# Attention stage of a macaron layer: order of the uses of one PSUM bank

## What is computed

```python
x = x + 0.5 * _L0_ffn_ref(_layernorm(x), ...)
x = x + _L0_attn_ref(_layernorm(x), ...)      # normalizes again, with ln_scale and ln_bias
x = x + 0.5 * _L0_ffn_ref(_layernorm(x), ...)

# _L0_attn_ref, h normalized:
c_q, c_kv = h @ w_down_q.T, h @ w_down_kv.T           # latents of 128
q, k, v = c_q @ w_up_q.T, c_kv @ w_up_k.T, c_kv @ w_up_v.T   # 16 heads of 64
q, k = rope(q), rope(k)
out = softmax(q k^T / 8) v;  out = out @ w_out.T + residual
```

## Time and profile before

| | |
|---|---|
| median of three runs | 4095.92 us (4093.1 to 4099.3) |
| profiled execution | 4098.04 us, span 4096.1 us |
| PE busy, whole span | 3897.4 us (95%), weight loads 2207.7 us (54%) |
| POOL, DVE, ACT busy | 2932.8 (72%), 2849.5 (70%), 2536.2 us (62%) |
| attention stage | about 520 to 3590 us |

### The profile page before, as it was taken

How to read it: one execution, slowest core, us unless ns; L and a number is a source line. 1 busy time by engine, 2 the same in 40 slices (tenths; PEclk the granted TensorE clock), 3 DMA queues, 4 the chain that set the end, 5 groups by cost and what they waited for, 6 DMA issues and landing times. The chain is left out here.

```text
span 4096.1 us, 65749 instructions
## 1 busy us (share of the span) xinstructions
PE 3897.4 (95%) x24908; PEld 2207.7 (54%) x24908; DVE 2849.5 (70%) x3796; ACT 2536.2 (62%) x3191; POOL 2932.8 (72%) x1632
## 2 busy tenths in 40 slices
PE   7999979999999999999999999999999999989999
PEld 6888834444444444444444444444444444478888
DVE  5656567777777776777778777767776777565563
ACT  4455446766766676667666766766676666645544
POOL 3444448878877897888788878878887888634443
PEclk9999989999999999999999999999999999999999
DMA  3233221111211221121122212211211121142331
GB/s 123 99 124 109 81 93 53 60 55 59 83 53 53 71 66 53 61 81 53 53 66 76 63 53 66 68 50 60 86 55 53 58 79 62 33 145 76 125 114 63
DMA packets 192772, 300.36 MB, mean 73 GB/s; under 512 B 50328, under 2 KB 100937, under 8 KB 191817
## 3 DMA queue, kind: packets, MB, share of 16 engines
q1 hardware_dynamic: 192456, 296.17, 22.3%
HBM read 201.20 MB, written 26.73 MB: 56 GB/s over the span
## 5 line engine op out<-in xcount | busy, mean ns | idle before, releaser
L1088 DVE TENSOR_REDUCE atNM<-atPS 128x2 f32<-128x1024 f32 x1024 | 1225.7, 1219 | 452.8 <-PE atPS L899 450.1
L1029 ACT ACTIVATE atPT<-atPS 128x1024 f32<-128x1024 f32 x1024 | 1014.0, 1024 | 773.1 <-PE atPS L920 766.7
L1187 POOL TENSOR_TENSOR atACC<-atACC,atPT 128x1024 f32<-128x1024 f32 x510 | 1238.7, 2429 | 89.3 <-ACT atPT L1029 39.1
L931 PE MATMUL atPO<-atPT,atV 128*64 128x512 f32 x4096 | 1014.2, 602 | 0.0
L1187 POOL TENSOR_TENSOR atACC<-atPT 128x1024 f32<-128x1024 f32 x255 | 606.6, 2379 | 262.8 <-PE atOT L953 181.7
L1020 ACT ACTIVATE atPS<-atSH 128x1024 f32<-128x1024 f32 x683 | 687.4, 1023 | 50.8 <-DVE atNM L1088 34.0
L920 PE MATMUL atPS<-atQH,atKL 64*128 64x512 f32 x2048 | 459.9, 445 | 66.3 <-DVE atPS L1094 51.7
L931 PEld LDWEIGHTS atPO<-atPT,atV 128*64 128x64 f32 x4096 | 259.0, 136 | 456.5 <-issue 433.1
L899 PE MATMUL atPS<-atKH,atQH 64*128 64x512 f32 x2048 | 444.0, 431 | 10.0 <-ACT atQH L1009 7.9
L1094 DVE COPY atPS<-atSH 128x1024 f32<-128x1024 f32 x341 | 418.7, 1228 | 37.9 <-DMA atSH<-atMD 11.4
L920 PE MATMUL atPS<-atQH,atKH 64*128 64x512 f32 x2048 | 406.6, 393 | 0.0
(11 more groups left out here) (278 smaller groups left out, 6461.5 us busy)
## 6 DMA issues: line engine op xcount, KB each, us to landing
atSH<-atMD SPq DMA_DIRECT2D x128, 512.0 KB, 4.3
atVT<-atR SPq DMA_DIRECT2D x508, 128.0 KB, 2.1
f1GB<-f1GD SPq DMA_DIRECT2D x128, 256.0 KB, 6.7
f2GB<-f2GD SPq DMA_DIRECT2D x128, 256.0 KB, 6.8
atRSUM<-atRD SPq DMA_DIRECT2D x126, 256.0 KB, 4.0
X<-x SPq DMA_DIRECT2D x4, 1024.0 KB, 6.0
XS<-x SPq DMA_DIRECT2D x16, 256.0 KB, 3.6
x<-X SPq DMA_DIRECT2D x16, 256.0 KB, 2.3
```

Source lines behind the costliest of these rows:

```text
L931: ins = pe.eng.matmul(PO[HI[h], :], V[n % 2][:, j, HI[h]], PT[k % NPT][:, h, :], start=j == 0, stop=j == T - 1)
L1029: act.eng.activation(PT[k % NPT][:, :, :], PS[ring.of[step]][:, :, :], ACT.Exp, scale=SCALE).then_inc(grown.sem)
L1088: dve.eng.tensor_reduce(NM[:, q // 4, :, q % 4, t], PS[ring.of[step]][:, :, :], AX.X, ALU.max, negate=True).then_inc(most_out.sem)
L1187: pool.eng.tensor_tensor(total[:, :, :], begun[:, :, :], PT[k % NPT][:, :, :], ALU.add).then_inc(gathered.sem)
```

## The change

Two things. A function `apart` looks at the tail of each pass: where the list at x + 1 has a raise and the list at x + 2 has any use of OT, the raise is taken out of its place between the two fills and put at the end of the pass, behind that use. And the last four entries of TURNS, for the second half of a batch, move: turns from periods -9 early and -9 late to -13 late and -12 late, latents from -8 early and -8 late to -9 late and -8 late.

```diff
-            TURNS = [(-21, late), (-20, late), (-17, early), (-17, late), (-9, early), (-9, late), (-8, early), (-8, late)]
+            TURNS = [(-21, late), (-20, late), (-17, early), (-17, late), (-13, late), (-12, late), (-9, late), (-8, late)]
@@
+            def uses(steps):
+
+                return [s for s in steps if s[0] in ("turn", "latent", "raise", "value", "row", "sum", "outward")]
+
+            def apart(one, two):
+
+                raised = [s for s in one if s[0] == "raise"]
+                if raised and uses(two):
+                    return [s for s in one if s not in raised], two + raised
+                return one, two
@@
-                order += others_of(x) + held + tile("attend", x - 1)
-                order += gathers(held + tile("attend", x - 1))
+                now = held + tile("attend", x - 1)
+                order += others_of(x) + now + gathers(now)
@@
-                order += tile("fill", x + 3) + others_of(x + 1) + tile("fill", x + 4) + now + gathers(now) + others_of(x + 2)
+                one, two = apart(others_of(x + 1), others_of(x + 2))
+                order += tile("fill", x + 3) + one + tile("fill", x + 4) + now + gathers(now) + two
```

## The result

The changed kernel takes 4137.6 us (median of 4 runs, 4136.2 to 4144.1) against 4097.0; the ratio is 1.0102, 95% interval 1.0088 to 1.0117. It is slower by 41 us; 4128 with a range of 4102 to 4146 was forecast. In the changed file every line behind the new functions stands 12 further down: 878 is now 890, 953 is 965, 1014, 996 and 1041 are 1026, 1008 and 1053.

The account below looks back on a forecast made before the run. PE's own matmul sequence was taken to bound the attention stage; 7.2 + 22.1 + 6.0 + 3.6 + 7.6 + 1.2 - 13.4 - 2.2 = +32 us on a median of 4095.9 gave 4128 us, range 4102 to 4146.

Parts of the forecast that it names:

- The frame: Attention stage, 520 to 3590 us: PE's own matmul sequence sets the time; an added stall counts unless later waits recover it.
- Rival 1: Slips of PE are taken back by shorter later waits for DVE fills: at most 23 us, 4105 us; chance 0.18.
- Case B: 21 tails, raise moved directly behind a row, waiting for ACT's copy after both fills: +1.05 each, +22.1 us.
- Case A: 20 tails, raise moved directly behind a sum, waiting for ACT's copy after both fills: +0.36 each, +7.2 us.
- the difference stays: Sum-then-raise tails with DVE late: fills and old wait are late together, so +0.36 still holds.
- case C: Five tails, two attends between raise and turn before; raise now directly behind the turn: 5 x 1.19, +6.0 us.
- case D: Five tails, one attend between raise and turn before; raise now directly behind the turn: +3.6 (two tails), +7.6 (three).
- four new turns with a raise two attends behind: Turn's copy falls between the two fills; bounds 0 and 0.78, 0.3 taken for each, +1.2 us.
- Turns and latents: Seven batches: two of three waits behind out-projections vanish, 14 x 0.96, -13.4; waits for fills used up, -2.2 us.
- new turns in slots with a wait for a fill: Five new turns land where PE waits for a DVE fill anyway, using up 0.45 each: -2.2 us.
- Cover: SyncE's later swap DMAs, POOL's rotate and DVE's raise operations stay covered after the move; nothing counted.
- margin of 0.1: DVE behind a moved raise: fill ready after 4.9 us, PE needs it after some 5.0; nothing counted.

Follow-up runs that it names:

- row run: Kernel before with old periods, a raise moved behind only where the later use is a row (21 tails): 4118.9 us, ratio 1.0049.
- the swap: Kernel before, raise and sum of a tail change places: 4081.1 us, ratio 0.9961; with the new periods 4071.5 (0.9935), on another chip 4068.9 (0.9931).

## Why the prediction was right, point by point

**The frame.** PE's own sequence sets the time and slips are not taken back: held. The row run moves 21 raises, loses 22.6 us in these tails and 20.2 in the stage, and nothing comes back in the passes directly behind (-0.1 us). Rival 1 (4105) would have given back about 0.45 a tail. The low share of weight loads, which spoke for it, did not show slack here: in an attend, matmuls start in pairs every 0.43 us, and the weight loads beside them take 0.14 of it.

**Case B, +22.1.** Measured +22.5 in the profiled run, 1.05 to 1.09 a tail for a forecast of 1.05; alone, +20 by the ratio. The mechanism is shown by the copy moved on ACT.

**Case A, +7.2.** Fourteen tails cost 0.28 to 0.45 for a forecast of 0.36, one nothing, and five 0.7 to 1.5, so that the sum is 10.8. The five are tails in which DVE was late and PE now stands still for 2.2 to 2.5 us. Two things failed there. In two of them (1.46 and 1.30) PE's clock is low inside the tail (below). In the other three (0.71, 0.76, 1.13) "the difference stays" is what failed: DVE's subtraction ahead of the reductions (line 1083, now 1095) took 2.77, 2.55 and 2.54 us where it had taken 2.48, 2.19 and 1.82 before, so the late tails are not late by the same amount in both executions, and the excess over 0.36 is about that difference.

**Cases C and D.** For the ten tails together, the moved turns included, the forecast comes to 6.0 + 3.6 + 7.6 + 5 x 0.58 = 20.1; measured 21.0. That this fits so well is partly luck. Without the turns' own time case C is 4.4 for 6.0 and case D 13.7 for 11.2. The waits themselves are as worked out: in the first D tail the raise starts 4.00 us after its old place, for 4.04 forecast, and in the C tail at 774.20 the next score comes 4.52 after that place, for 4.49. But three of the five C passes had a stall of some 0.55 ahead of their tail that is gone in this execution, and four of the five D tails have a low clock in them or behind them. The four new turns with a raise two attends behind cost about 0.7 each, not 0.3: with 0.78 as the upper bound I had gone for the wrong end; +1.6.

**Turns and latents, -13.4 and -2.2.** The passes that lost a turn or a latent gave -21.9, of which 14 x 0.58 = 8.1 is the turns' own time: -13.8; the latents among them only change places. The new turns in slots with a wait for a fill cost nothing, where 0.13 each had been left. The periods alone gave -13.9. That one latent per batch stays behind an out-projection was right, seven waits.

**Cover.** SyncE and POOL: right, no wait of PE for either came up. DVE behind the moved raise, with the margin of 0.1: held. The passes directly behind the 21 rows of the row run do not grow. Those behind the five D tails grew by 3.6 us in all, but by 0.5 to 1.4 only behind the four with a low clock, and by -0.01 behind the one without; in the run with `apart` alone, whose two D tails have no low clock, it is 0.01 in sum.

**Sum.** 32 forecast, 41 measured, at the upper end of the forecast's own range of 4115 to 4138; the sign, the mechanism and the sizes of the main terms hold. The largest thing missing is PE's clock, for which the sum has no term. A stretch of 3.4 us at the lower clock costs 1.4 to 1.6 us (below); the profiled execution after has nine of them between 620 and 3590 us, that before has three, so about 9 of its 42.8 us are the clock (an estimate, 6 x 1.5). The run with `apart` alone checks the rest: it has three such stretches like the kernel before, and its stage grew by 35.9 us, where the forecast's terms for it, 7.2 + 22.1 + 3 x 1.19 + 2 x 1.82, add up to 36.5.

## What to carry to other kernels

Before a use of a shared bank is moved right behind another, look up which engine empties the bank and what stands in that engine's queue at that moment; the wait is not only the copy's 0.3 to 0.8 us but also the time until the copy's turn comes. A listed wait is not a gain in reserve: work that lay ahead of it was free, and moving that work behind the wait's place pays for it anew. The cure for a bank passed from hand to hand is distance and a place in an idle stretch of the emptying engine, here the sum ahead of the first fill with two attends behind it, 16 us on top of the exchange of places and, with the new periods, 46 us in all against the kernel before.

## What the hardware showed that I had not expected

A wait of about 2 us or more can cost more than itself. After the wait of 2.34 us for a turn's copy, the raise ran in 1.98 us; in the same kind of tail at 1990.74, behind a wait as long, in 1.08:

```profile
830.07 0.66 PE L872 MATMUL atOT<-ident,Y 128*128 128x128 f32 x4
833.06 1.98 PE L890 MATMUL atOT<-atCKV,WK 128*64 128x512 f32 x4 [2.34 <-ACT atHT L1008]
834.97 0.80 PE L932 MATMUL atPS<-atQH,atKL 64*128 64x512 f32 x2
...
1990.74 1.08 PE L890 MATMUL atOT<-atCKV,WK 128*64 128x512 f32 x4 [2.33 <-ACT atHT L1008]
```

The granted clock of PE in such stretches of the kernel after (length, busy us of PE, PEld, DVE, ACT, POOL, clock, DMA share, GB/s):

```profile
833.00:836.40 3.40, 3.34 (x10) 1.46 (x12) 1.29 (x2) 0.01 (x1) 0.51 (x1) 0.50 0.00 0
...
1307.00:1313.00 6.00, 5.14 (x18) 2.43 (x18) 2.41 (x3) 1.83 (x3) 1.48 (x1) 0.54 0.11 44
...
2311.00:2314.00 3.00, 2.64 (x8) 0.94 (x10) 0.62 (x2) 1.28 (x3) 0.53 (x1) 0.50 0.03 5
2707.00:2710.00 3.00, 2.76 (x8) 1.05 (x10) 0.74 (x2) 0.19 (x1) 0.71 (x1) 0.50 0.03 3
3140.00:3143.00 3.00, 3.00 (x12) 1.44 (x14) 1.29 (x2) 0.00 (x0) 0.35 (x1) 0.56 0.02 5
```

The clock falls to its lower level, 1.2 of 2.4 GHz, eight times between 620 and 3590 us, seven times for 3.4 us and once for 6.8. Twelve of the moved raises wait 2.2 to 2.5 us, seven behind a sum and five behind a turn, and all eight drops start at one of the twelve or within 2 us behind it; none lies at one of the 39 shorter waits, and four of the twelve have none. In the kernel before there are three drops in this stretch, each right behind one of its six waits of 1.9 to 2.1 us at a sum; the first:

```profile
1293.49 1.06 PE L953 MATMUL atOT<-atACC,atones 128*32 128x512 f32 x8 [2.08 <-DVE atU L1072]
```

```profile
1295.00:1298.00 3.00, 3.00 (x14) 1.73 (x14) 1.71 (x2) 1.78 (x3) 3.00 (x2) 0.50 0.01 3
```

Over all kept runs the picture is the same. Between 620 and 3520 us six of them have PE waits of more than 1.85 us, 47 in all, with 27 drops, each at one of these waits or within 2 us behind it. In the five others (ACT's copies moved forward, the swap with and without the new periods, the sum ahead of the fill) no wait is longer than 1.4 us, and the clock does not fall once. What decides whether a given wait is followed by a drop is not shown.

What a drop costs shows when the pass behind the tail is counted too. Two D tails with two new turns and a drop grew, with the pass behind, by 4.66 and 4.70 us, the third of this kind, without a drop, by 3.13 (2.55 + 0.58 = 3.13 were reckoned); the other two D tails, with a drop, by 3.36 and 3.25, for 1.8 in the run with `apart` alone, where they have none. Two passes in which only the kernel before has a drop became 1.53 and 1.54 shorter. So it is 1.4 to 1.6 us each. How many drops the unprofiled executions had is not recorded; their mean clock is, and it does not explain why the profiled one took 6.5 us more than the median: it has 0.985, and the others (4137.7, 4136.2, 4137.6 us) have 0.985, 0.987 and 0.986.
